# Scaling of the third normalisation as 32 ScalarE instructions a chunk instead of one VectorE instruction

## The chip, the core and the metric

The kernel runs on one core of a Trainium2 chip. The metric is the device time of one execution in microseconds (us), the median of several runs. The engines of the core are TensorE (PE), VectorE (DVE), ScalarE (ACT), GpSimd (POOL) and SyncE (SP, which only issues transfers). Each engine works through its own list of instructions in the order in which they are written and stops at a wait until the semaphore has reached the count that is asked for.

## The reference, cut to what matters

Four residual layers work on an input of 256 images, 256 channels and 7 x 7 positions in float32, each on a group-normalised copy of its input (32 groups of 8 channels):

```
x = x + L0(gn(x))      # 1x1 convolution with gathered rows of the weight
x = x + L1(gn(x))      # linear attention over heads, 5x5 depthwise convolution, projection
x = x + L2(gn(x))      # spatial gate: arg max, gaussian, sigmoid
x = x + L3(gn(x))      # attention over the 49 positions of an image
def gn(v): (g - mean(g)) / sqrt(var(g) + 1e-5)   # for each image and each group
```

The change concerns the last `gn`: `z3 = (x3 - mean3) * rstd3`, whose result feeds L3 (its products f, g and hh, and the residual term).

## The kernel before, in words

Channels lie on partitions (KT = 2 tiles of 128). A chunk is NB = 16 images, COLS = 784 columns a tile (49 positions by 16 images), so that one full tensor of a chunk is 128 x 1568. There are 16 chunks. The first two phases (set-up, L0 and L1) are not touched. The third phase, `gate_and_attention_phase`, does L2 and L3 as a software pipeline that is written out by hand: body r runs the steps of chunk r for `intake`, r-1 for `norm2`, r-2 for `gate`, r-3 for `norm3`, r-4 for `attend` and r-5 for `leave`, for r from 0 to 20. So `norm3` is in bodies 3 to 18 and `attend` in bodies 4 to 19; body 18 has `norm3` and `attend` but neither `norm2` nor `gate`. The order of the work is the order of the `run(...)` lines in `v_body`, `pe_body`, `a_body` and `g_body`.

The third normalisation goes: `v_sum` (DVE sums x3), `pe_stat` (PE spreads the sums over groups), `v_mean`, `v_centre` (zc[1] = x3 - mean, L995), `a_square` (ACT), `v_square_sum` (L1008), `pe_stat`, `v_var` (L1012), `g_root` (POOL raises to the power -0.5, L1436), and `v_scale` (L1023), which writes z3, one of two buffers. In each chunk rstd is 128 x 2 tiles x 16 images: one value for each partition, tile and image.

Who reads z3: `pe_fg` of the next body (L1267, its first step), `pe_hh` (L1290) and the identity products of `pe_out` (L1307). Near the place of the change the orders are:

- DVE, end of a body: `v_x3`, `v_scale` of z2, `v_gap`, `v_scale` of z3, `v_x4` part 0 (L1160, waits for `pe_out` part 0). Then, in the next body: `v_sum` of x3 (L982), `v_hot` (L1043 on, waits for ACT's s_sb), `v_x4` part 1, `v_mean` (L988, waits for `pe_stat`).
- ACT, end of a body: `a_exp` (L1391), `a_hh` 1 and 2, `a_sim_square`, `a_tanh` (L1373, the gate), `a_hh` 3 (L1398), `a_beta` (L1404, two instructions), `a_sums` (L1352, s_sb).
- PE, end of a body: `pe_gate` (L1225), `pe_hh` 3 (L1290), `pe_turn` (L1300, first half after `a_hh` 2, second half after `a_hh` 3), `pe_out` 0, `pe_sums` (L1219), `pe_out` 1; next body: `pe_fg`, `pe_gap` (L1219), `pe_stat` (L1204) for the means, `pe_hot` and so on.
- POOL: `g_root` of norm3, `g_deviation` (L1448), `g_root` of norm2, `g_gapped` (L1443).

Of the kernel before, what the change touches and what calls it, by code (L numbers as in the profile page):

```python
# [13 lines left out]
S = HW * HW  # L14
NB = 16
# [3 lines left out]
KT = C // 128  # L19
# [15 lines left out]
def settle(eng, met):  # L35


    eng.sem_inc(met, 1)
# [787 lines left out]
def gate_and_attention_phase(nc, bass, mybir, W, x2, out, ins, chunks):  # L826
# [10 lines left out]
    ACT = mybir.ActivationFunctionType  # L837
# [5 lines left out]
    with ctx:  # L843
        def sb(name, shape):
            return ctx.enter_context(nc.sbuf_tensor(name, shape, f32))
# [12 lines left out]
        def normed(it, k):  # L858

            return x2_in if k == 0 else x3[it % 3]  # L860

        def scaled(it, k):

            return z2 if k == 0 else z3[it % 2]

        x4 = sb("x4", [128, KT, COLS])
        zc = [sb("zc2", [128, KT, COLS]), sb("zc3", [128, KT, COLS])]
        z2 = sb("z2", [128, KT, COLS])
        z3 = [sb("z3_0", [128, KT, COLS]), sb("z3_1", [128, KT, COLS])]
# [4 lines left out]
        rstd = [sb("rstd2", [128, KT, NB]), sb("rstd3", [128, KT, NB])]  # L874
# [63 lines left out]
        def done(ins_, name):  # L938
            return ins_.then_inc(sems[name], 1)

        def wait(eng, name, count):

            if not isinstance(count, int) or count > 0:
                eng.wait_ge(sems[name], count)

        def by_image(ap):
            return ap.rearrange("p t (b s) -> p t b s", b=NB)

        def over_positions(ap):
            return ap.unsqueeze(3).to_broadcast([128, KT, NB, S])  # L950
# [15 lines left out]
        def two_images(ap, n):  # L966

            return ap[:, PR * n:PR * n + PR]
# [22 lines left out]
        def v_centre(v, it, k):  # L991
            wait(v, f"mean{k + 2}", it + 1)

            wait(v, f"z{k + 2}", it)
            done(v.tensor_tensor(by_image(zc[k][:, :, :]), by_image(normed(it, k)[:, :, :]),  # L995
                                 over_positions(mean[k][:, :, :]), ALU.subtract), f"centred{k + 2}")
            if k == 0:

                wait(v, "gapm", it)
                done(v.scalar_tensor_tensor(gapc[:, :], stat[0][:, :], 1.0 / S,  # L1000
                                            mean[0][:, :, :].rearrange("p t b -> p (t b)"),
                                            ALU.mult, ALU.subtract), "gapc")
# [12 lines left out]
        def v_scale(v, it, k):  # L1015
            wait(v, f"rstd{k + 2}", it + 1)
            if k == 0:

                wait(v, "gated", 2 * it)
            else:  # L1020

                wait(v, "o_mm", 4 * it - 4)
            done(v.tensor_tensor(by_image(scaled(it, k)[:, :, :]), by_image(zc[k][:, :, :]),  # L1023
                                 over_positions(rstd[k][:, :, :]), ALU.mult), f"z{k + 2}")

        def v_then(v, it, ins_, name):

            done(ins_, name)
            wait(v, name, it + 1)
# [133 lines left out]
        def v_body(v, intake, norm2, gate, norm3, attend, leave):  # L1163

            def run(step, chunk, *more):
                if chunk is not None:
                    step(v, chunk, *more)

            run(v_sum, norm3, 1)
            run(v_hot, gate)  # L1170
            run(v_x4, leave, 1)
            run(v_mean, norm3, 1)
            run(v_mean, norm2, 0)
            run(v_centre, norm3, 1)
            run(v_picked, gate)
            run(v_centre, norm2, 0)
            run(v_square_sum, norm3, 1)
            run(v_dist, gate)
            run(v_var, norm3, 1)
            run(v_max, attend)  # L1180
            run(v_dsum, gate)
            run(v_sim, gate)
            run(v_spread_of_sim, gate)
            run(v_square_sum, norm2, 0)
            run(v_context, gate)
            run(v_var, norm2, 0)
            run(v_probs, attend)
            run(v_sum, intake, 0)
            run(v_x3, gate)
            run(v_scale, norm2, 0)  # L1190
            run(v_gap, norm2)
            run(v_scale, norm3, 1)
            run(v_x4, attend, 0)


# [63 lines left out]

        def pe_fg(pe, it):  # L1260

            wait(pe, "z3", it + 1)

            wait(pe, "x4_ok", 2 * it - 1)
            for t in range(KT):
                for h in range(2):
                    mm = pe.matmul(p_a[2 * G * h:2 * G * h + 2 * G, 0, 0:HALF], W["wqk"][:, t, :],  # L1267
                                   z3[it % 2][:, t, HALF * h:HALF * h + HALF], start=(t == 0), stop=(t == KT - 1))
            done(mm, "fg_mm")
# [9 lines left out]

        def pe_hh(pe, it, n):  # L1280

            wait(pe, "z3", it + 1)
            if n < 2:

                wait(pe, "x4_ok", 2 * it)
            else:
                wait(pe, "hh_ev", 4 * it + n - 1)
            for q in range(2):
                for t in range(KT):
                    mm = pe.matmul(p_b[0:PR, n % 2, C * q:C * q + C], two_images(z3[it % 2][:, t, :], 2 * n + q),  # L1290
                                   W["wv"][:, t, :], start=(t == 0), stop=(t == KT - 1))
                done(mm, "hh_mm")
# [114 lines left out]
        def a_body(a, intake, norm2, gate, norm3, attend, leave):  # L1407
            def run(step, chunk, *more):
                if chunk is not None:
                    step(a, chunk, *more)  # L1410

            run(a_fg, attend)
            run(a_gap, gate)
            run(a_square, norm3, 1)
            run(a_hh, attend, 0)
            run(a_square, norm2, 0)
            run(a_gauss, gate)
            run(a_exp, attend)
            run(a_hh, attend, 1)
            run(a_hh, attend, 2)  # L1420
            run(a_sim_square, gate)
            run(a_tanh, gate)
            run(a_hh, attend, 3)
            run(a_beta, attend)
            run(a_sums, norm2)


        def g_root(g, it, k):

            wait(g, f"var{k + 2}", it + 1)  # L1430

            wait(g, f"z{k + 2}", it)
            if k == 0:
                wait(g, "gapm", it)
            settle(g, sems["met_g"])
            done(g.tensor_tensor(rstd[k][:, :, :].rearrange("p t b -> p (t b)"), var[k][:, :], W["minus_half"][:, :],  # L1436
                                 ALU.pow), f"rstd{k + 2}")
# [86 lines left out]
        @block.scalar  # L1524
        def _(a):
            done(a.activation(log_norm[:, :], W["theta"][:, 2:3], ACT.Ln), "logged")
            a.wait_ge(sems["params"], 5)
            bodies(a, a_body)
# [6 lines left out]
def program(nc, ins, out, chunks, n_classes):  # L1535
    import concourse.bass as bass
    from concourse import mybir
    from contextlib import ExitStack
    f32 = mybir.dt.float32
    x2 = nc.dram_tensor("x2_scratch", (chunks, 128, KT, COLS), f32, kind="Internal").ap()  # L1540
    xpart = nc.dram_tensor("x1_scratch", (chunks, 128, KT, COLS), f32, kind="Internal").ap()
    qt = nc.dram_tensor("qkv_scratch", (2, PR, NP, 3 * C), f32, kind="Internal").ap()
    agg = nc.dram_tensor("agg_scratch", (2, NP, 3 * C, PR), f32, kind="Internal").ap()
    ctx = ExitStack()
    with ctx:
        W = {}
        for name, shape in (
            ("w_qkv", [128, KT, 3 * C]), ("w_proj", [128, 4, C]), ("wv", [128, KT, C]), ("wqk", [128, KT, 64]),
            ("w_sub", [128, KT, C]), ("b_sub", [128, KT]), ("mask8", [128, 128]), ("mask_vo", [128, VO]),
            ("ident", [128, 128]), ("image_of", [PR, 2]), ("bn_scale", [128, KT]), ("bn_shift", [128, KT]),  # L1550
            ("g_par", [64, 4]), ("theta", [64, 3]), ("gamma", [128, 1]),
            ("minus_half", [128, KT * NB]), ("plus_half", [64, NB // 2]),
        ):
            W[name] = ctx.enter_context(nc.sbuf_tensor(name, shape, f32))
        setup_phase(nc, bass, mybir, ins, W, n_classes)
        layer_one_phase(nc, bass, mybir, ins, W, (qt, agg, xpart, x2), chunks)
        gate_and_attention_phase(nc, bass, mybir, W, x2, out, ins, chunks)
# [90 lines left out]
```

## Time and profile before

| what | value |
|---|---|
| median of 3 runs | 2461.83 us (2460.21, 2461.83, 2505.93) |
| the profiled execution | 2472.42 us, its span 2470.6 us |
| PE busy | 1950.4 us (79%) |
| DVE busy | 1413.4 us (57%) |
| ACT busy | 928.5 us (38%) |
| POOL busy | 274.7 us (11%) |
| mean granted TensorE clock | 0.898 of full speed |

The shares are averages over two very different parts. In 40 slices of the span DVE is busy five tenths or less up to about 70% of the span (set-up, L0 and L1), and eight or nine tenths in the last 30%, which is the phase that the change touches: it begins near 1755 us and a body of it takes some 41 us in the middle. PE is busy seven tenths there, ACT two to three.

### The profile page before, as it was taken

What the parts mean: (1) busy time and instruction counts of PE and PEld (TensorE: products, weight loads), DVE (VectorE), ACT (ScalarE), POOL (GpSimd) and SP (SyncE); (2) the same over time, 40 slices, a digit from 0 to 9 for tenths busy, and PEclk for the clock granted to TensorE, in tenths of its full rate; (3) what the DMA queues carried; (4) which work ended last, traced back from release to release, by engine and by line L of the source; (5) the groups of instructions that cost most, each with busy time, mean ns of one, the idle gap of its engine ahead of it and who ended that gap; (6) DMA issues with size and microseconds to landing.
All of it is one profiled execution on the core that took longest, in us unless ns stands there. A gap on an engine that the chain in (4) does not pass through costs nothing. (4 is left out here: it accounts for less than half of the span.)

```text
span 2470.6 us, 40333 instructions
## 1 busy us (share of the span) xinstructions
PE 1950.4 (79%) x15572; PEld 1244.2 (50%) x15572; DVE 1413.4 (57%) x2847; ACT 928.5 (38%) x2181; POOL 274.7 (11%) x77
## 2 busy tenths in 40 slices
PE   2788888889999899978687888888436877676768
PEld 1344444445555565556566666666114444343435
DVE  4556565655545545322222244444489989899984
ACT  0344443444444444433333344444113232323232
POOL 1000000000000000000000000000143434343430
PEclk9889999999999999988888899999658888888889
DMA  2111112264675763788889755553111121212101
GB/s 90 51 67 66 66 66 79 80 149 108 180 188 152 198 181 103 194 197 203 214 194 213 191 144 132 131 132 93 70 52 53 53 66 53 66 53 66 56 36 40
DMA packets 258675, 279.42 MB, mean 113 GB/s; under 512 B 207092, under 2 KB 233076, under 8 KB 254392
## 3 DMA queue, kind: packets, MB, share of 16 engines
q1 hardware_dynamic: 258328, 276.58, 41.1%
q8 instruction: 128, 2.10, 0.3%
q14 instruction: 59, 0.48, 0.1%
q0 software_dynamic: 160, 0.26, 0.0%
HBM read 161.21 MB, written 115.61 MB: 112 GB/s over the span
## 5 line engine op out<-in xcount | busy, mean ns | idle before, releaser
L484 DVE TENSOR_TENSOR vk<-p_vk,mask_vo 128x512 f32<-128x512 f32 x256 | 177.1, 692 | 725.1 <-PE p_vk L378 725.0
L1436 POOL TENSOR_TENSOR rstd<-var,minus_half 128x32 f32<-128x32 f32 x32 | 173.9, 5435 | 2062.3 <-DVE var L1012 2062.3
L414 PE MATMUL p_dw<-tw,qd 98*64 98x98 f32 x3072 | 244.6, 296 | 95.9 <-DMA tw<-in_w_toep 56.5
L414 PEld LDWEIGHTS p_dw<-tw,qd 98*64 98x64 f32 x3072 | 200.2, 205 | 151.9 <-issue 48.2
L624 ACT ACTIVATE agg_out<-p_dw 128x294 f32<-128x294 f32 x256 | 106.5, 416 | 317.3 <-PE p_dw L414 294.1
L597 ACT ACTIVATE half_b<-p_qkv 98x384 f32<-98x384 f32 x256 | 125.8, 491 | 258.6 <-PE p_qkv L337 258.4
L337 PE MATMUL p_qkv<-w_qkv,half_a 128*98 128x384 f32 x512 | 198.0, 535 | 0.0
L437 PE MATMUL p_g<-o,w_proj 128*128 128x392 f32 x512 | 195.6, 506 | 0.5 <-ACT o L632 0.5
L337 PE MATMUL p_qkv<-w_qkv,z_odd 128*98 128x384 f32 x512 | 187.8, 512 | 0.0
L390 PE MATMUL p_out<-vk,qr 128*49 128x136 f32 x2048 | 170.7, 287 | 1.3 <-DVE oN L499 1.1
L616 ACT ACTIVATE qr<-p_turn 128x196 f32<-128x196 f32 x256 | 85.4, 334 | 197.1 <-PE p_turn L347 116.5
L1290 PE MATMUL p_b<-wv,z 128*98 128x256 f32 x512 | 147.7, 446 | 0.4 <-ACT hh L1398 0.4
L430 PE MATMUL p_g<-half_a,w_sub 128*128 128x392 f32 x256 | 107.3, 548 | 36.3 <-DVE half_a L549 36.3
L632 ACT ACTIVATE o<-p_turn 128x196 f32<-128x196 f32 x256 | 85.4, 334 | 116.1 <-PE p_turn L399 115.5
L337 PEld LDWEIGHTS p_qkv<-w_qkv,half_a 128*98 128x98 f32 x512 | 88.7, 184 | 73.2 <-issue 73.2
L1204 PE MATMUL p_wide<-stat,mask 128*128 128x32 f32 x128 | 27.4, 317 | 119.6 <-DVE stat L1008 83.4
L1290 PEld LDWEIGHTS p_b<-wv,z 128*98 128x98 f32 x512 | 96.2, 196 | 48.7 <-issue 16.5
L390 PEld LDWEIGHTS p_out<-vk,qr 128*49 128x49 f32 x2048 | 111.6, 126 | 16.6 <-issue 1.7
L378 PEld LDWEIGHTS p_vk<-vT,kT 98*32 98x32 f32 x4096 | 70.6, 109 | 97.4 <-issue 65.8
L337 PEld LDWEIGHTS p_qkv<-w_qkv,z_odd 128*98 128x98 f32 x512 | 84.6, 176 | 67.2 <-issue 67.2
L437 PEld LDWEIGHTS p_g<-o,w_proj 128*128 128x128 f32 x512 | 91.2, 193 | 53.3 <-issue 14.1
L603 ACT ACTIVATE vT<-half_b,image_of 98x256 f32<-98x256 f32 x256 | 114.7, 498 | 0.0
(179 smaller groups left out, 3294.3 us busy)
## 6 DMA issues: line engine op xcount, KB each, us to landing
qkv_scratch<-half_b SPq DMA_DIRECT2D x32, 1176.0 KB
qd<-qkv_scratch SPq DMA_DIRECT2D x16, 2352.0 KB
agg_scratch<-agg_out SPq DMA_DIRECT2D x64, 588.0 KB, 7.1
tw<-in_w_toep SPq DMA_DIRECT2D x128, 220.5 KB
x_scratch<-xb SPq DMA_DIRECT2D x32, 784.0 KB, 5.3
half_a<-agg_scratch SPq DMA_DIRECT2D x48, 392.0 KB, 6.4
half_b<-agg_scratch SPq DMA_DIRECT2D x48, 392.0 KB, 6.0
half_a<-in_x SPq DMA_DIRECT2D x16, 784.0 KB, 4.5
```

The lines of the kernel that those rows point to most:

```text
L337: mm = pe.matmul(p_qkv[r][0:PR, 0:QKV], z[c % 2][:, t, PR * w:PR * w + PR], W["w_qkv"][:, t, QKV * e:QKV * e + QKV], start=(t == 0), stop= ...
L390: mm = pe.matmul(out_of[64 * i:64 * i + S, pr, 0:VO], qr[:, G % 4, at:at + S], vk[:, G % 2, pr, i, :], start=True, stop=True)
L414: mm = pe.matmul(p_dw[NP * cp:NP * cp + NP, PR * s:PR * s + PR], qd[:, QB % 2, :, ch - QB_CH * qb], tw[:, SB % 2, :, 6 * (F % SB_FILLS) + ...
L430: mm = pe.matmul(bank[:, 0:HALF], W["w_sub"][:, t, 128 * m:128 * m + 128], y[:, t, HALF * h:HALF * h + HALF], start=(t == 0), stop=(t == K ...
L437: mm = pe.matmul(bank[:, 0:HALF], W["w_proj"][:, q0 + e, 128 * m:128 * m + 128], o[:, n % 2, e, HALF * h:HALF * h + HALF], start=(e == 0), ...
L484: v.tensor_tensor(dst[:, :, 0:128].rearrange("p k (c n) -> p k c n", c=HC), src[:, :, 0:2 * D].unsqueeze(2).to_broadcast([128, 4, HC, 2 * D]),
L597: a.activation(raw[:, e, w, :], p_qkv[r][0:PR, 0:QKV], ACT.Copy).then_inc(raw_ev, 1)
L603: a.activation(vT[:, G % 2, :, i, :, 0:2 * D], src.rearrange("r q (c n) -> r q c n", c=HC), ACT.Copy, scale=W["image_of"][:, i:i + 1]).the ...
L616: a.activation(qr[:, G % 4, :], p_turn[:, 0:2 * PR], ACT.Relu).then_inc(qr_ok, 1)
L624: a.activation(agg_out[:, DB % 2, at:at + 3, :].rearrange("p s n -> p (s n)"), p_dw[:, 0:3 * PR], ACT.Copy).then_inc(dw_ev, 1)
L1290: mm = pe.matmul(p_b[0:PR, n % 2, C * q:C * q + C], two_images(z3[it % 2][:, t, :], 2 * n + q), W["wv"][:, t, :], start=(t == 0), stop=(t ...
L1436: done(g.tensor_tensor(rstd[k][:, :, :].rearrange("p t b -> p (t b)"), var[k][:, :], W["minus_half"][:, :], ALU.pow), f"rstd{k + 2}")
```

## The change

The step `v_scale` for norm3 is taken out of DVE's list. A new step `a_scale3(t)` on ACT does the same product in 16 instructions for each tile t, one for each image: a copy of 128 x 49 elements with a scale that is read from one column of rstd. Tile 0 is placed between `a_tanh` and `a_hh` 3, tile 1 between `a_beta` and `a_sums`. The semaphore z3 now counts KT * NB = 32 for a chunk instead of 1; `pe_fg`, `pe_hh`, `v_centre` and `g_root` wait for the new counts.

```
         def v_centre(v, it, k):
-            wait(v, f"z{k + 2}", it)
+            wait(v, f"z{k + 2}", it if k == 0 else KT * NB * it)
...
+        def a_scale3(a, it, t):
+            if t == 0:
+                wait(a, "rstd3", it + 1)
+                wait(a, "o_mm", 4 * it - 4)
+            for b in range(NB):
+                done(a.activation(z3[it % 2][:, t, S * b:S * b + S], zc[1][:, t, S * b:S * b + S], ACT.Copy,
+                                  scale=rstd[1][:, t, b:b + 1]), "z3")
...
             run(v_gap, norm2)
-            run(v_scale, norm3, 1)
             run(v_x4, attend, 0)
...
         def pe_fg(pe, it):
-            wait(pe, "z3", it + 1)
+            wait(pe, "z3", KT * NB * (it + 1))
...
         def pe_hh(pe, it, n):
-            wait(pe, "z3", it + 1)
+            wait(pe, "z3", KT * NB * (it + 1))
...
             run(a_tanh, gate)
+            run(a_scale3, norm3, 0)
             run(a_hh, attend, 3)
             run(a_beta, attend)
+            run(a_scale3, norm3, 1)
             run(a_sums, norm2)
...
         def g_root(g, it, k):
-            wait(g, f"z{k + 2}", it)
+            wait(g, f"z{k + 2}", it if k == 0 else KT * NB * it)
```

## Rows read from the trace of the kernel before

**Rows 1.** Line 1023 by source: duration ns min/median/max, first and last start.

```profile
L1023 DVE TENSOR_TENSOR z<-zc,rstd x32: 1781/1784/1792, 1773.9 to 2436.7; 128x1568 f32<-128x1568 f32 x32
```

**Rows 2.** Chain that ended last, in order of time: start us, us, what; one body.

```profile
2074.04 5.37 POOL rstd L1436
...
2082.11 0.72 ACT gate L1373
...
2085.95 3.11 PE p_b L1290 x8
2089.08 0.61 ACT hh L1398
...
2101.09 0.58 PE p_wide L1204 x4
2101.80 1.78 DVE zc L995
```

**Rows 3.** Timeline of DVE, same body: start, us, instructions, [idle before <-releaser].

```profile
2091.37 1.78 DVE L1023 TENSOR_TENSOR z<-zc,rstd 128x1568 f32<-128x1568 f32 x1
2093.50 0.97 DVE L1160 TENSOR_TENSOR x<-p_a,x 128x784 f32<-128x784 f32 x1 [0.35 <-PE p_a L1310]
...
2096.09 0.54 DVE L1043 TENSOR_REDUCE best<-s_sb 64x8 f32<-64x392 f32 x1
...
2101.47 0.41 DVE L988 TENSOR_SCALAR mean<-p_wide 128x32 f32<-128x32 f32 x2 [1.59 <-PE p_wide L1204]
```

**Rows 4.** Timeline of ACT, same body, the places where the new steps go.

```profile
2089.08 0.60 ACT L1398 ACTIVATE hh<-p_b 98x512 f32<-98x512 f32 x1 [6.25 <-PE p_b L1290]
...
2090.31 0.50 ACT L1404 ACTIVATE beta<-p_b 98x392 f32<-98x392 f32 x1 [0.24 <-PE p_b L1300]
2094.95 0.49 ACT L1352 ACTIVATE s_sb<-p_group 64x392 f32<-64x392 f32 x1 [4.14 <-PE p_group L1219]
```

**Rows 5.** Timeline of PE: the first reader of z3, and one product at two clocks.

```profile
2068.06 2.83 PE L1219 MATMUL p_group<-prod,sel 128*32 128x392 f32 x8 [2.86 <-DVE prod L1082]
...
2098.11 1.54 PE L1267 MATMUL p_a<-z,wqk 128*64 128x392 f32 x8
2099.58 1.51 PE L1219 MATMUL p_group<-gapped,sel 128*32 128x392 f32 x8
```

**Rows 6.** Timeline of ACT: its smallest instructions of this phase, one after the other.

```profile
2073.77 0.39 ACT L1361 ACTIVATE dist<-dist,inv_scale 64x112 f32<-64x112 f32 x1 [2.52 <-DVE dist L1072]
2074.19 0.39 ACT L1363 ACTIVATE gauss<-dist,log_norm 64x112 f32<-64x112 f32 x1
2074.95 1.98 ACT L1391 ACTIVATE sc<-p_a,neg_max 98x98 f32<-98x98 f32 x8 [0.38 <-DVE neg_max L1146]
```

**Rows 7.** Groups of ACT by form over the span: busy us, mean ns | idle before.

```profile
L1348 ACT ACTIVATE sq<-zc 128x1568 f32<-128x1568 f32 x32 | 48.3, 1510 | 92.6 <-DVE zc L995 92.6
...
L649 ACT ACTIVATE std<-var 128x32 f32<-128x32 f32 x32 | 7.2, 224 | 6.3 <-DVE var L532 6.3
```

**Rows 8.** Timeline of DVE where body 3 ends.

```profile
1846.32 1.78 DVE L1023 TENSOR_TENSOR z<-zc,rstd 128x1568 f32<-128x1568 f32 x1
...
1849.76 0.55 DVE L1043 TENSOR_REDUCE best<-s_sb 64x8 f32<-64x392 f32 x1
```

**Rows 9.** Timeline of ACT, same place.

```profile
1849.23 0.49 ACT L1352 ACTIVATE s_sb<-p_group 64x392 f32<-64x392 f32 x1 [10.60 <-PE p_group L1219]
```

**Rows 10.** Timeline of all engines in body 18 and at the start of body 19.

```profile
2431.26 5.44 POOL L1436 TENSOR_TENSOR rstd<-var,minus_half 128x32 f32<-128x32 f32 x1 [24.37 <-DVE var L1012]
...
2436.76 0.60 ACT L1398 ACTIVATE hh<-p_b 98x512 f32<-98x512 f32 x1 [1.63 <-PE p_b L1290]
...
2437.41 0.54 PE L1300 MATMUL p_b<-ident,sc 98*98 98x98 f32 x4 [0.35 <-ACT hh L1398]
...
2437.99 0.50 ACT L1404 ACTIVATE beta<-p_b 98x392 f32<-98x392 f32 x1 [0.24 <-PE p_b L1300]
...
2444.18 1.54 PE L1267 MATMUL p_a<-z,wqk 128*64 128x392 f32 x8
```

**Rows 11.** Busy time and PEclk of a stretch: PE, PEld, DVE, ACT, POOL, clock, DMA, GB/s.

```profile
2068.00:2072.00 4.00, 3.22 (x11) 0.97 (x12) 3.90 (x7) 1.51 (x1) 0.00 (x0) 0.59 0.34 58
```

**Rows 12.** Chain that ended last, body 5: the first p_b product after the gate.

```profile
1920.16 3.66 PE p_b L1290 x8
```

## The prediction

> **What bounds the kernel now.** The page says that DVE is 80 to 90% busy in the phase that the change touches, which invites the sum "one instruction of 1.78 us less on the busiest engine, in 16 chunks". The first view to read is therefore not a share but the chain that ended last, over one body in the middle. It goes from DVE's centring through the first half of the body to POOL's root, on to the gate on ACT, then to PE's p_b product, ACT's copy of hh, and from there along PE to the p_wide product, which releases DVE's next centring [rows 2]. L1023 is not on it: from 2085.95 to 2101.67 the body belongs to PE, with one ACT copy between. The second view is DVE's own timeline over that stretch [rows 3]: right behind z3 DVE waits 0.35 us for PE's p_a, and before the mean it waits another 1.59 us for PE's p_wide. An engine that waits for PE directly behind the instruction that is removed gains nothing when that instruction goes. The third view is ACT's timeline, which shows the two holes that the new steps are put into [rows 4]: 6.25 us between the gate and hh, 4.14 us between beta and s_sb. The fourth is the beginning and the end of the phase, where bodies are incomplete and the holes may be absent [rows 8 to 10].
>
> **The change, part by part.**
>
> *Removed from DVE:* 16 of the 32 instructions of L1023, each 1784 ns [rows 1]; busy time falls by 16 x 1.78 = 28.5 us. In the shown body z3 starts at 2091.37. Without it DVE stands at x4 part 0 some 1.7 us sooner, but that waits for p_a and still starts at 2093.50; its idle time grows from 0.35 to about 2.05 us [rows 3]. What follows on DVE does not move. Saved on the path: 0 in bodies 4 to 17. In body 3, where nothing attends yet, the chain does run through z3 at 1846.32. But DVE's best, two instructions on at 1849.76, needs ACT's s_sb, which ends at 1849.23 + 0.49 = 1849.72 whatever DVE does [rows 8, 9]: saved at most 0.04 us. So the removal is worth 0, and PE's wait is what covers it.
>
> *Added to ACT:* 32 copies of 128 x 49 a chunk, 512 in all. No row shows this form. Four rows bound it. The eight exponentials of 98 x 98, each with its own bias column, take 1.98 us together: 0.25 us each. Two instructions of 64 x 112, the second of which waits for the first, start 0.42 us apart [rows 6]. An instruction of 128 x 32 out of and into SBUF takes 224 ns, and 1568 columns take 1510 ns, so a column costs (1510 - 224) / 1536 = 0.84 ns [rows 7]; 49 columns are then 0.24 us. I take 0.24, since the SBUF row of 32 columns is nearest in size and the exponentials, nearest in kind (independent, back to back, a pointer operand, a semaphore count each), say the same. 16 of them are 3.8 us. The ends are 0.20 (the exponentials less 49 columns at 0.84 ns) and 0.42, so 3.2 to 6.7 us for a tile.
>
> *Tile 0, bodies 4 to 17:* rstd3 is ready at 2074.04 + 5.37 = 2079.41, before the gate ends at 2082.83 [rows 2], so the new wait costs nothing. Behind the new instructions on ACT stand hh, beta and s_sb; for hh PE waits. The hole is 6.25 us [rows 4], 0.39 us an instruction: at 0.24 the step ends 2.4 us before hh is due. Cost 0, covered by PE's gate and p_b products; without that cover it would be the whole 3.8 us. The wait on o_mm asks for products of the body before, done long ago.
>
> *Tile 1, bodies 4 to 17:* from 2090.81 the hole to s_sb is 4.14 us [rows 4], 0.26 us an instruction. At 0.24 it just fits. Beyond 0.26 s_sb comes late, but DVE's best reads it at 2096.09, 0.65 us after it is ready, and behind that lies DVE's 1.59 us before the mean [rows 3], which absorbs a delay too: 4.14 + 0.65 + 1.59 = 6.38 us, 0.40 us an instruction, before the mean is late. The reader of z3 itself, PE's p_a product at 2098.11 [rows 5], is 7.3 us away. Cost 0. The counts that DVE's centring and POOL's root now wait for are reached some 7 and 20 us ahead.
>
> Set against the ScalarE page of the Trainium skill ("ScalarE: Activation LUTs", section "Rules for kernel authors"): it budgets about 0.3 us for an ACTIVATE with a pointer operand plus 0.83 ns an element, and tells authors to leave multiplications to VectorE. By that, as an estimate, a tile would be 16 x 0.34 = 5.5 us. It would still fit hole one, overrun hole two by 1.3 us, of which 0.65 us is free at best and the rest goes into the wait before the mean; only the end of the kernel, below, would cost 1.7 us more. The column price agrees with the 0.84 ns above; the 0.3 us does not agree with 0.25 us an exponential [rows 6].
>
> *Body 18:* here is neither gate nor norm2, and the hole is gone. rstd3 ends only at 2431.26 + 5.44 = 2436.70, and hh, which stands behind the new tile 0 on ACT, started at 2436.76 [rows 10]. Now ACT waits for rstd3, scales 3.8 us, and hh starts near 2440.6. PE's second half of the turn waited for that hh already (0.35 us), and everything to the end hangs on it: **+3.8 us** on the path. Tile 1 starts after beta, near 2438.5 + 3.8 = 2442.3, ends 2446.1, and PE's p_a product, at 2444.18 before, comes at 2448 or later: hidden.
>
> In addition PE stands still for about 4 us instead of 0.35 us. What follows such a stop is shown in the middle of each body: after 2.86 us of waiting the 8 products of L1219 take 2.83 us, at a granted clock of 0.59 (a mix of 1.2 and 2.4 GHz), where the same 8 products in a busy stretch take 1.51 us [rows 5, 11]. I add that difference once, **+1.3 us**; the bounds are 0 (the clock stays up) and 3 us (the outputs of body 18, some 6 us, half of them at the lower level).
>
> **Sum:** 0 + 0 + 3.8 + 1.3 = +5.1 us on the profiled execution's 2472.42, that is 2477.5 us. The median lies 10.6 us below the profiled execution; the same difference on 2461.83 gives **2467 us**, +0.2%.
>
> **The rivals.**
>
> *A, the forecast:* chance 0.73; own range 2464 to 2472, from +3.2 with no clock loss to +6.7 with 3 us of it.
>
> *B, DVE is the bound after all.* If the waits behind z3 were only slack that re-forms further back, each of 15 bodies would be 1.70 us shorter (z3's start after z2's): -25 us, 2437 us. For it: 90% busy, and the first half of the body is DVE's. Against it: the wait for PE directly behind z3 in each full body, and a chain without L1023. 0.05.
>
> *C, slower: the small copies are dear, and hh is late in every body.* Place: tile 0 in front of hh. Point: above 6.25 / 16 = 0.39 us. Price: 14 x (16p - 6.25) + 16p + 1.3 us. At the 0.42 us of the dependent pair it is 14 x 0.47 + 6.7 + 1.3 = 14.6 us, 2476. For 2% (49 us) p must be 0.56 us, more than any ACT row of up to 128 columns above. 0.10, of which 0.02 beyond 2%.
>
> *D, the clock.* PE's p_b product behind the gate takes 3.11 us in the middle of the phase but 3.66 us in body 5 [rows 2, 12]: bodies that do the same work differ by how the low stretch of the clock falls on them. If a shift near body 3 moved it in all 14 full bodies it would be up to 14 x 0.55 = +7.7 us; if the early ones improved, -2 or -3 us. With the 5.1 us: 2464 to 2475. Against it: nothing on PE moves before body 18. 0.12.
>
> **Range and chances.** 2457 to 2480 holds A and D whole and most of C, and a few us for run-to-run spread (two runs before are 1.6 us apart); B and the far end of C are left out. Over 2% means under 2412.6 or over 2511.1, about what a measurement can tell from no change: faster 0.01 (no case reaches it), within 0.96, slower 0.03 (the far part of C and a disturbed median like the run of 2505.93).
>
> **What would show each step.** In the trace after: full bodies still near 41 us; DVE's wait before x4 part 0 near 2 us; ACT's new instructions near 0.24 us apart, tile 0 ended before hh is due; s_sb at its old place to within half a microsecond; in body 18 hh some 3.8 us late behind rstd3, and PE at a lower clock after it. The forecast is wrong if bodies shorten, if they lengthen because hh starts right behind a new copy, or if body 18 costs nothing.

## The result, and the profile after

The changed kernel takes 2475.53 us (median of 16 runs) against 2462.61 us before (16 runs): a ratio of 1.0050, 95% interval 1.0036 to 1.0065, that is +12.3 us with 8.9 to 16. The 12.3 us are the ratio times the time before; one disturbed run of each kernel (3411.15 us after, 2505.93 us before) is in the medians but not in the ratio. The change makes the kernel slower by half a per cent, well inside 2%; the forecast was +5.1 us. The profiled execution took 2480.26 us (span 2478.5), 7.8 us more than the one before; it reached the first centring of the phase at 1758.17 us instead of 1762.09, in a part that is the same in both kernels. So the two traces are compared by stretches of the phase, each from one centring of DVE (L995) to another; the phase itself is 11.8 us longer.

The page after has the new group on ACT (its columns: busy us, mean ns of one, idle before):

```profile
L1031 ACT ACTIVATE z<-zc,rstd 128x49 f32<-128x49 f32 x512 | 118.9, 323 | 1.6 <-POOL rstd L1445 1.6
```

The timeline of ACT over one full body shows both holes of [rows 4] with what now stands in them:

```profile
2077.89 0.71 ACT L1380 ACTIVATE gate<-sim,half_par 64x392 f32<-64x392 f32 x1 [3.54 <-DVE sim L1123]
2078.51 3.72 ACT L1031 ACTIVATE z<-zc,rstd 128x49 f32<-128x49 f32 x16
2085.40 0.60 ACT L1405 ACTIVATE hh<-p_b 98x512 f32<-98x512 f32 x1 [3.17 <-PE p_b L1297]
...
2086.63 0.50 ACT L1411 ACTIVATE beta<-p_b 98x392 f32<-98x392 f32 x1 [0.25 <-PE p_b L1307]
2087.03 3.72 ACT L1031 ACTIVATE z<-zc,rstd 128x49 f32<-128x49 f32 x16
2091.27 0.49 ACT L1359 ACTIVATE s_sb<-p_group 64x392 f32<-64x392 f32 x1 [0.52 <-PE p_group L1226]
```

Sixteen copies take 3.72 us. In front of hh 3.17 us are still free, in front of s_sb 0.52 us: neither is late. The timeline of DVE, the counterpart of [rows 3]:

```profile
2089.82 0.97 DVE L1168 TENSOR_TENSOR x<-p_a,x 128x784 f32<-128x784 f32 x1 [2.59 <-PE p_a L1317]
...
2097.79 0.41 DVE L988 TENSOR_SCALAR mean<-p_wide 128x32 f32<-128x32 f32 x2 [1.59 <-PE p_wide L1211]
```

The wait right behind the place of z3 has grown from 0.35 to 2.59 us, more than the 1.70 that were freed, because in this body PE's products in front of hh ran longer (3.70 us against 3.11 in [rows 2]). PE's timeline:

```profile
2081.66 3.70 PE L1297 MATMUL p_b<-wv,z 128*98 128x256 f32 x8
```

The body shown is body 9 in both traces; it takes 41.56 us after and 40.98 before. Other early bodies differ the other way (body 4: 40.93 after, 41.91 before), and body 15 takes 40.96 us in both. Nothing was won. Where the time went is seen at the end. ACT and PE in body 18, two timelines, against [rows 10]:

```profile
2433.60 3.73 ACT L1031 ACTIVATE z<-zc,rstd 128x49 f32<-128x49 f32 x16 [1.60 <-POOL rstd L1445]
2437.23 0.57 ACT L1405 ACTIVATE hh<-p_b 98x512 f32<-98x512 f32 x1
```

```profile
2437.86 0.89 PE L1307 MATMUL p_b<-ident,sc 98*98 98x98 f32 x4 [3.93 <-ACT hh L1405]
2438.54 1.56 PE L1314 MATMUL p_a<-z,ident 128*128 128x392 f32 x2
2439.90 1.87 PE L1317 MATMUL p_a<-beta,hh 98*128 98x98 f32 x8
...
2450.74 2.88 PE L1274 MATMUL p_a<-z,wqk 128*64 128x392 f32 x8
```

The same products of body 18 before, from PE's timeline:

```profile
2437.80 0.93 PE L1307 MATMUL p_a<-z,ident 128*128 128x392 f32 x2
2438.56 1.03 PE L1310 MATMUL p_a<-beta,hh 98*128 98x98 f32 x8
```

And the clock in that part of the trace after (start and end of the stretch, its length, then PE, PEld, DVE, ACT, POOL busy; granted clock; DMA; GB/s), where 0.50 is 1.2 GHz and 1.00 is 2.4:

```profile
2435.00:2437.00 2.00, 0.00 (x0) 0.00 (x0) 0.00 (x0) 2.00 (x10) 0.00 (x0) 0.94 0.00 0
2439.00:2441.00 2.00, 2.00 (x8) 1.44 (x7) 0.00 (x0) 2.00 (x10) 0.00 (x0) 0.50 0.03 8
2438.00:2453.00 15.00, 15.00 (x52) 10.79 (x52) 1.95 (x2) 4.30 (x18) 0.00 (x0) 0.50 0.03 10
```

ACT waits 1.60 us for rstd3, copies for 3.73 us, and only then takes hh; PE stands still for 3.93 us, its clock falls, and it stays at 1.2 GHz although PE is busy without a gap until the p_a product ends at 2453.62. The ledger, all from starts and ends in the two traces:

| stretch | before | after | difference |
|---|---|---|---|
| bodies 4 to 17 (centring to centring) | 572.1 | 572.5 | +0.4 |
| body 18: centring to start of hh 3 | 11.55 | 15.15 | +3.6 |
| start of hh 3 to end of the p_a product | 8.96 | 16.39 | +7.4 |
| end of the p_a product to end of span | 24.89 | 24.84 | -0.1 |

The remaining 0.4 us of the phase's 11.8 lie ahead of body 4.

### The profile page after: what moved, and what is told of

Same layout as the page of the kernel before. It is cut to its first block and busy times, and to the rows that moved or that the text cites. A ratio compares the mean times of both kernels' runs of the same rounds, so it can differ in the third digit from the quotient of the medians.

```text
span 2478.5 us, 40829 instructions
## 1 busy us (share of the span) xinstructions
PE 1955.6 (79%) x15572; PEld 1248.0 (50%) x15572; DVE 1386.6 (56%) x2831; ACT 1044.3 (42%) x2693; POOL 254.0 (10%) x77
## 3 DMA queue, kind: packets, MB, share of 16 engines
q1 hardware_dynamic: 258328, 276.58, 40.9%
## 5 line engine op out<-in xcount | busy, mean ns | idle before, releaser
L616 ACT ACTIVATE qr<-p_turn 128x196 f32<-128x196 f32 x256 | 85.4, 334 | 197.4 <-PE p_turn L347 116.4
L632 ACT ACTIVATE o<-p_turn 128x196 f32<-128x196 f32 x256 | 85.4, 334 | 116.0 <-PE p_turn L399 115.3
L1297 PEld LDWEIGHTS p_b<-wv,z 128*98 128x98 f32 x512 | 97.1, 198 | 49.0 <-ACT z L1031 15.5
L1031 ACT ACTIVATE z<-zc,rstd 128x49 f32<-128x49 f32 x512 | 118.9, 323 | 1.6 <-POOL rstd L1445 1.6
L390 PEld LDWEIGHTS p_out<-vk,qr 128*49 128x49 f32 x2048 | 111.2, 126 | 16.5 <-issue 1.8
```

Of the source, the lines that this page charges most:

```text
L390: mm = pe.matmul(out_of[64 * i:64 * i + S, pr, 0:VO], qr[:, G % 4, at:at + S], vk[:, G % 2, pr, i, :], start=True, stop=True)
L616: a.activation(qr[:, G % 4, :], p_turn[:, 0:2 * PR], ACT.Relu).then_inc(qr_ok, 1)
L1031: done(a.activation(z3[it % 2][:, t, S * b:S * b + S], zc[1][:, t, S * b:S * b + S], ACT.Copy, scale=rstd[1][:, t, b:b + 1]), "z3")
```

## The experiments

Each was timed beside the kernel before on the same chip. The "tail" is the stretch in its trace from the centring of body 17 to the end of the span: 82.2 us before, 93.2 us after. "Bodies" is the stretch of bodies 4 to 17: 572.1 and 572.5. Body 17 (36.8 us) is in both columns. The column "us" is the ratio times the time before. The expectations of e3b and e6 count the tail to DVE's last instruction, 3.8 us sooner: 78.3 before and 89.3 after.

| run | ratio, 95% interval | us | bodies | tail |
|---|---|---|---|---|
| e1 last chunk on DVE | 0.9985 (0.9969 to 1.0000) | -3.7 | 572.9 | 82.2 |
| e2 before, hh late in body 18 | 1.0036 (1.0018 to 1.0053) | +8.9 | 572.9 | 93.2 |
| e3 20 products in the stop | 1.0043 (1.0024 to 1.0063) | +10.6 | 572.9 | 93.3 |
| e3b 6 products in the stop | 1.0013 (0.9997 to 1.0029) | +3.2 | 572.2 | 85.7 |
| e4 removal alone | 0.9983 (0.9965 to 1.0001) | -4.2 | 569.0 | 82.2 |
| e5 both tiles before hh 3 | 1.0101 (1.0067 to 1.0134) | +24.9 | 583.1 | 92.2 |
| e6 hh late by half | 1.0008 (0.9989 to 1.0027) | +2.0 | 573.5 | 85.6 |
| e7 reordered, z3 on ACT | 1.0079 (1.0054 to 1.0104) | +19.5 | 578.8 | 97.7 |
| e8 reordered, z3 on DVE | 1.0079 (1.0057 to 1.0102) | +19.5 | 578.6 | 97.7 |
| e9 both tiles behind beta in body 18 | 1.0007 (0.9991 to 1.0022) | +1.7 | 572.1 | 85.4 |
| e10 PE filled, z3 on DVE | 0.9933 (0.9915 to 0.9950) | -16.5 | 552.4 | 78.8 |
| e11 PE filled, z3 on ACT | 0.9959 (0.9941 to 0.9977) | -10.1 | 557.2 | 83.1 |

**e1, the last chunk on DVE.** In `a_scale3` and in `v_body`:

```
+            if it == chunks - 1:
+                return
...
             run(v_gap, norm2)
+            run(v_scale_last, norm3)     # as v_scale, last chunk alone, counts 32
```

> The changed kernel, but z3 of the last chunk (body 18) is scaled by DVE in one instruction as before; the other 15 chunks stay on ACT. Theory T (all the loss is in body 18: hh 3.6 us late behind rstd3, then TensorE at 1.2 GHz to the end of the body): the last body is as before, so the time is that of the kernel before, within 2 us, and from the last centring to the end of the span 48 us become some 41 plus the store. Theory U (each of the 14 full bodies loses 0.5 to 0.9 us by the copies or the clock): the loss stays at 8 us or more. Theory B (DVE gives something back in each body): faster than before by up to 25 us.

The loss is gone with one chunk of 16 changed (the 48 and 41 us in the expectation were misread: from the last centring to the end of the span it is 56.4 us after and 45.4 here and before). The tail is that of before and the bodies keep their length with z3 on ACT. Theory U falls, and B with it. The median is 3.7 us under the kernel before, with an interval that ends at 1.0000; the trace has no stretch that is shorter, so nothing is claimed from it.

**e2, the delay alone.** The kernel before with this in front of `a_hh` 3:

```
+        def a_fill(a, it):
+            if it == chunks - 1:
+                wait(a, "rstd3", it + 1)
+                for b in range(NB):       # 16 copies into sq[0], which is free then
```

> The kernel before, z3 on DVE throughout, with 16 small ACT copies into an unused tile in front of hh 3 in body 18 alone, behind a wait for rstd3. Theory T: this alone gives the whole loss of the change, +11 to +13 us: hh about 3.6 us late, PE idle near 4 us, then the second half of the turn, the outputs and the p_a product (7.9 us before) at 1.2 GHz in some 15 us. If the clock counted for little: +3.8 us. Theory U: at most +4 us.

The tail is 93.2 us, that of the changed kernel to a tenth, without any other part of the change; the median is +8.9 us (4.4 to 13). PE's timeline repeats what it did after:

```profile
2428.76 0.89 PE L1300 MATMUL p_b<-ident,sc 98*98 98x98 f32 x4 [3.93 <-ACT hh L1398]
2429.45 1.56 PE L1307 MATMUL p_a<-z,ident 128*128 128x392 f32 x2
...
2441.64 2.88 PE L1267 MATMUL p_a<-z,wqk 128*64 128x392 f32 x8
```

So 11.0 us in the trace come from one late instruction, in one body.

**e3 and e3b, PE kept busy.** The changed kernel, between the halves of `pe_turn`, with 20 and then 6 in `range`:

```
+                if h == 1 and it == chunks - 2:
+                    for r in range(6):
+                        pe.matmul(p_group[0:G, 0, 0:HALF], sel[:, 0, :], ...)   # read by nobody
```

> The changed kernel; while PE waits for the late hh in body 18 it computes 20 products of 128 x 392 that nobody reads (between the halves of the turn). hh stays 3.6 us late. Theory T: the granted clock stays at 1.00, the last body loses 3.6 to 4 us and no more, so the time is 7 to 8 us under the changed kernel and 4 to 5 us over the one before. If the slow outputs had another cause than PE's stop (the copies on ACT, for one), the time is that of the changed kernel.

> As e3_pe_kept_busy, where 20 products took 13.35 us (two passes each, 0.33 us a pass) and not 3.9, so that it kept the clock at 1.00 but added 10 us of its own. Now 6 products, 4.0 us, the length of PE's stop. Theory T: the clock stays at 1.00 through the outputs of body 18 and only the 3.6 to 4 us of the late hh are left: from the first centring of body 17 to the end of the span 82 to 83 us, against 89.3 in the changed kernel and 78.3 before; in the median 7 us under the changed kernel. If the low clock came from ACT's copies and not from PE's stop: no change from 89.3.

In e3 the filler was mis-sized: a float32 product shows as two passes, 20 of them took 13.35 us instead of 4, and its time says nothing; only that the clock stayed at 1.00. In e3b the filler fits the stop. PE's timeline:

```profile
2427.22 4.14 PE L1307 MATMUL p_group<-z,sel 128*32 128x392 f32 x12
2431.28 0.54 PE L1311 MATMUL p_b<-ident,sc 98*98 98x98 f32 x4
2431.66 0.86 PE L1318 MATMUL p_a<-z,ident 128*128 128x392 f32 x2
2432.36 1.03 PE L1321 MATMUL p_a<-beta,hh 98*128 98x98 f32 x8
```

and its clock:

```profile
2430.00:2434.00 4.00, 4.00 (x22) 2.38 (x20) 0.00 (x0) 3.68 (x15) 0.00 (x0) 1.00 0.00 0
```

ACT still copies during the outputs (3.68 us busy), hh is as late as in the changed kernel, but the outputs are as fast as before. The tail is 85.7 us: 3.6 more than before, 7.4 less than after. This splits the loss: 3.6 us the late hh, 7.4 the clock. The clock falls here because PE stands still, not because ACT is busy: the two kernels differ in nothing but the six products.

**e6, half the delay.** e2 with `range(NB // 2)`.

> As e2_before_delay18 with 8 copies in place of 16: hh 1.8 us late, PE's stop about 2.1 us instead of 3.9. If the clock's loss grows in proportion to the stop: half of the loss, +5.5 us, 83.8 us from the centring of body 17 to the end. If a stop of 2.1 us is short enough to leave the clock up: +1.8 us, 80.2 us. In proportion to nothing (any stop costs all): +9 us.

PE's stop is 2.12 us and the tail 85.6, +3.4 us: 1.8 of delay and 1.6 of clock. PE's timeline shows the low level over the first products only:

```profile
2428.76 0.54 PE L1300 MATMUL p_b<-ident,sc 98*98 98x98 f32 x4 [2.12 <-ACT hh L1398]
...
2430.31 1.86 PE L1310 MATMUL p_a<-beta,hh 98*128 98x98 f32 x8
...
2433.11 1.03 PE L1310 MATMUL p_a<-beta,hh 98*128 98x98 f32 x8
```

Between two of the three expectations, +1.8 and +5.5 us: a short stop does cost clock, but less than in proportion.

**e9, the copies moved.** In body 18 alone both tiles stand behind `a_beta`.

> The changed kernel; in body 18 alone both tiles stand behind beta, so hh 3 does not wait for rstd3. All scaling stays on ACT. Theory T: hh is on time, PE does not stop there; z3 is complete 7.4 us after beta, some 1.8 us after the p_a product could start, so PE stops about 1.8 us there instead: before +2 us, plus at most 2 us if the clock falls after it. If only the amount of work on ACT mattered: as the changed kernel.

+1.7 us (-2.2 to +5.4), tail 85.4, +3.2 us: hh is on time, PE stops 1.52 us for z3 in front of p_a, and its next long run of hh products takes 9.72 us instead of 8.84. The same copies on the same engine cost less than a third of what they cost in front of hh (3.2 of 11.0 us).

**e5, the cover taken away.** Both tiles in front of `a_hh` 3 in every body.

> The changed kernel with both tiles in front of hh 3 in every body: 32 copies, 7.4 us, in a hole of 6.3 to 6.8 us. Theory T (the hole is the cover, and behind it hh is on the path): each of the 14 full bodies is 0.6 to 1.2 us longer, and body 18 is late by another 3.7 us: 12 to 21 us over the changed kernel. If hh had more room than the forecast says: +3.7 us, from body 18 alone.

ACT's timeline of a full body:

```profile
2158.84 7.33 ACT L1031 ACTIVATE z<-zc,rstd 128x49 f32<-128x49 f32 x32
2166.08 0.57 ACT L1405 ACTIVATE hh<-p_b 98x512 f32<-98x512 f32 x1
```

hh now starts right behind the last copy. The 14 bodies are 11.0 us longer than before, 0.8 each, within the 0.6 to 1.2 that were expected from the size of the hole. The time is +24.9 us (16.5 to 33, from four runs), 12.6 over the changed kernel. In body 18 PE stands still 7.5 us, but the low clock behind it costs only 2.0 us (from PE's restart behind hh to the end of p_a 10.3 instead of 8.3), so the tail is 92.2, less than after. The stop is twice as long as in the changed kernel and the clock's part a quarter.

**e4, the removal alone.** DVE scales one image of z3 only, ACT gets nothing.

```
-            done(v.tensor_tensor(by_image(scaled(it, k)[:, :, :]), ...
+                done(v.tensor_scalar(z3[it % 2][:, 0, 0:S], zc[1][:, 0, 0:S], rstd[1][:, 0, 0:1], None, ALU.mult), "z3")
```

> The removal alone: in the kernel before, DVE scales only the first image of z3 (128 x 49, about 0.2 us instead of 1.78), the rest of z3 stays at zeros written once at the start of the phase; nothing is added to ACT. The attention is then computed on other data. Theory T (PE's wait covers L1023): 0 to -2 us, DVE's wait in front of x4 part 0 grows from 0.35 to about 1.9 us. Theory B (DVE bounds the bodies): -20 to -25 us.

```profile
2121.88 0.24 DVE L1023 TENSOR_SCALAR z<-zc,rstd 128x49 f32<-128x49 f32 x1
2123.99 0.97 DVE L1162 TENSOR_TENSOR x<-p_a,x 128x784 f32<-128x784 f32 x1 [1.87 <-PE p_a L1312]
```

DVE's timeline: 1.54 us less work, 1.52 us more waiting, as forecast (1.9). The body of that time is 40.96 us, as before. -4.2 us with an interval that touches 1.0001; the 3.1 us fewer in "bodies" lie in the early ones: bodies 4 to 9 took 40.9 each here, while in each other trace with the body's order of before some of them took 41.5 to 42.4, with z3 on either engine (rival D). That the early bodies differ by the clock and not by the removal is argued from those other traces, not tested. Theory B's -20 to -25 is excluded.

**e7 and e8, a shorter path.** `v_body` and `a_body` reordered, with z3 on ACT (e7, last chunk on DVE) and on DVE (e8):

```
             run(v_picked, gate)
-            run(v_centre, norm2, 0)
             run(v_square_sum, norm3, 1)
             run(v_dist, gate)
             run(v_var, norm3, 1)
-            run(v_max, attend)
+            run(v_centre, norm2, 0)
...
             run(v_var, norm2, 0)
+            run(v_max, attend)
```

> Built on e1_last_on_dve. The path of a body runs through the first half of DVE's list, so two steps that the gate does not need leave it: the maximum of the scores goes behind the variance of norm2 (ACT's exponentials behind the tanh), and the centring of norm2 behind the variance of norm3, so that POOL's root starts earlier. Of the 32 copies 8 stand before hh 3 and 24 behind beta. Theory T: the gate is ready 1.05 us sooner in each of 14 full bodies, which DVE's waits at the end of the body (2.6 and 1.6 us) can give: -15 us against e1. If POOL's root or another wait takes its place: 0.

> The same new order built on the kernel before, with z3 on DVE throughout. DVE then has 1.7 us less room at the end of a body (waits of 0.35 and 1.6 us), which still holds the 1.2 us that x4 part 0 comes late. Theory T: -15 us against the kernel before, the same as on ACT, so that moving z3 to ACT is worth nothing even then. If the room on DVE is what decides: the version with z3 on ACT is 10 us or more faster than this one.

Wrong, in sign: +19.5 us, both. Timelines of DVE and POOL in e8:

```profile
2102.70 1.77 DVE L995 TENSOR_TENSOR zc<-x,mean 128x1568 f32<-128x1568 f32 x1
...
2111.40 0.16 DVE L1113 TENSOR_SCALAR sstd<-sstd 64x8 f32<-64x8 f32 x1 [0.61 <-POOL sstd L1448]
...
2115.61 0.97 DVE L1150 TENSOR_REDUCE ssm<-sc 98x8 f32<-98x784 f32 x1 [2.04 <-ACT sc L1391]
```

```profile
2102.99 6.79 POOL L1436 TENSOR_TENSOR rstd<-var,minus_half 128x32 f32<-128x32 f32 x1 [15.40 <-DVE var L1012]
```

POOL's root, now beside DVE's centring, takes 6.79 us instead of 5.44 [rows 10], and DVE, which had hidden the exponentials behind other work, waits 2.04 us for them. Bodies 4 to 15 take about 41.8 us each in both. In both traces the chain that ended last goes through that wait to z of norm2, and from there over PE's sums of it (L1219) to the next mean: it leaves DVE just ahead of z3, so that z3's engine makes no difference here either. It is close, though: in e8 DVE has no wait left from the exponentials to the next centring, where in e7 it still waits 1.68 us before the mean. The tail is 15.5 us longer. In both of its last bodies PE stands still 3.14 us until DVE has scaled the exponentials, which now come late on ACT, and in body 18 the first groups of output products behind the stop take 1.87 us instead of 1.03; what each part costs was not separated.

**e10 and e11, the low clock in each body.** Before the second statistics product of norm2 PE stands still 5.6 us in every body with a gate, and the gate's products and hh 3 then run at a mean granted clock of 0.55 (2082 to 2089 us before). Seven products that nobody reads go there:

```
+        def pe_fill(pe, it):
+            wait(pe, "sim_max", it + 1)
+            for r in range(7):
+                pe.matmul(p_group[0:G, 0, 0:HALF], sel[:, 0, :], ...)
...
+            run(pe_fill, gate)
             run(pe_stat, norm2, 0, 1)
```

> The kernel before, with 7 products of 128 x 392 (two passes of 0.33 us each, 4.7 us in all, read by nobody) in PE's 5.6 us stop in front of the second statistics product of norm2, in each of the 16 bodies with a gate. They should keep TensorE at 2.4 GHz for the gate's products and for hh 3, which would be 2.65 us sooner (the products 1.5 instead of 3.0 us, hh 3 1.94 instead of 3.1). With z3 on DVE only the waits of DVE behind it can be given back, 0.35 + 1.59 = 1.9 us a body: -27 us in all. If the clock stays low all the same: 0.

> The same 7 products on e1_last_on_dve (z3 on ACT but for the last chunk), 8 of the 32 copies before hh 3 and 24 behind beta, since the hole before hh 3 shrinks to 3.6 us. Here DVE's waits are 2.6 and 1.6 us, so the whole 2.65 us of PE can be given back: -37 us against the kernel before, 10 us faster than e10. That would be the place where the change is worth something: with PE out of the way DVE bounds the end of the body. If DVE does not bound it even then, both are the same.

e10 is the fastest kernel of the study, -16.5 us (12 to 21 less), 0.67% under the kernel before and some 29 us under the changed one. PE's timeline of a body in which the filler holds the clock, beside [rows 2]:

```profile
2106.22 4.80 PE L1297 MATMUL p_group<-z,sel 128*32 128x392 f32 x14
...
2112.08 0.93 PE L1225 MATMUL p_wide<-gate,spread 32*128 32x392 f32 x4 [0.73 <-ACT gate L1380]
2112.82 0.85 PE L1225 MATMUL p_group<-gate,spread 32*128 32x392 f32 x4
2113.60 1.97 PE L1290 MATMUL p_b<-wv,z 128*98 128x256 f32 x8
```

That body is 39.3 us long; in the body before it p_b still took 3.73 us behind the same filler, and it was 41.2. Over 14 bodies the gain is 19.7 us of the 27 expected; ahead of body 4 the kernel loses 2.7 us, which leaves 17.0 for the phase. e11 was to be 10 us faster than e10 and is not; its best body is 39.3 us as well. Further on in the same body of e10, PE's timeline shows why:

```profile
2120.80 1.51 PE L1219 MATMUL p_group<-z,sel 128*32 128x392 f32 x8 [0.81 <-DVE z L1023]
```

PE now waits for z of norm2, which DVE makes just ahead of z3, and the chain that ended last leaves DVE there, with z3 on either engine. DVE bounds these bodies, but not behind z3, so moving z3 cannot shorten them. In the longer bodies PE comes last, as before. The two kernels also differ otherwise: the clock falls in other bodies in e11, its other order of copies (8 and 24) brings s_sb up to 1.3 us late, for which DVE waits 0.31 to 0.56 us in nine bodies, and from the centring of body 18 on e11 is 2.6 us longer.

## Why the prediction was right or wrong

- *The removal from DVE, 0 on the path:* right. DVE's wait grew in its place (after: 2.59 us; e4: 1.87), and a body of 40.96 us is 40.96 or 40.97 in before, after, e1 and e4. The chain and the wait behind the instruction told more than the 90% of busy time.
- *The price of a copy, 0.24 us:* 3.72 us for 16, 0.23 each; the sum had 3.8. Taking the start-to-start distance of the exponentials instead of a duration mattered: the page's mean is 323 ns for one, and 16 x 0.323 would be 5.2 us, yet they overlap. The estimate of 0.34 us from the Trainium skill ("ScalarE: Activation LUTs", section "Rules for kernel authors") is near the duration of one and too high for sixteen in a row.
- *Tile 0 and tile 1 in bodies 4 to 17, 0:* right, +0.4 us over 14 bodies in the trace. The point of 0.39 us an instruction was confirmed from the other side by e5: 7.3 us in the hole lengthen each body by 0.8.
- *Body 18, +3.8 us by the late hh:* right, 3.6 in the trace, 3.6 in e3b.
- *The clock, +1.3 us with a bound of 3:* this is the term that was mis-sized. It measured 7.4 us (after and e2), against 1.6 behind a stop of 2.1 us (e6) and 2.0 behind one of 7.5 us (e5). The prediction priced it by one group of products at a mean clock of 0.59 [rows 5, 11] and bounded it by "half of the outputs", as if the low level had to end while PE was busy with the outputs; here all outputs and the p_a product, nearly 16 us of busy PE, ran at 1.2 GHz. The bound should have been the whole busy stretch at half speed, 8 us.
- *The rivals:* B is excluded by e1 and e4. C did not occur; its mechanism is real (e5), its price per copy was not. The forecast's own range, rival A with 2464 to 2472, missed: its ends, +3.2 and +6.7 us, give 2465 to 2468.5, and +12.3 lies outside both. D's spread is visible in every trace: bodies 4 to 17 take 569.0 to 573.5 us in the kernels whose bodies have the order and the cover of before, independent of z3's engine.
- *The total:* 2467 forecast, 2475.5 measured, inside the range of 2457 to 2480; +5.1 against +12.3, and 6.1 of the 7.2 us between them are the clock term. That the total falls inside is partly luck: the upper end was put at 2480 for the rivals C and D, and neither of them made the loss. The phase of the two profiled executions differs by 11.8 us, the medians by 12.9, the ratio says 12.3.

What stays open is why the clock stayed low for nearly 16 us behind a stop of 3.9 us and for 5 us or less behind stops of 2.1 and 7.5 us. The runs show it depends on more than the stop's length; e2 repeats the long one with the same work before it.

## What to carry to other kernels

Before moving work off a busy engine, look at what that engine does right behind the instruction: if it waits there for another engine, the move is worth nothing, however busy the engine is on average. Then walk through the bodies in which the pipeline is half empty, since the hole that hides the moved work may not exist there; one body of 21 cost the whole difference here, and leaving its chunk on the old engine took it back (e1). And price a new stop of TensorE not by its length alone but also by what all the work behind it would cost at half the clock.

## What the runs showed of the hardware that was not expected

DVE's instructions slow POOL's, and not the other way round: g_gapped (128 x 1568 on POOL) takes 4.30 us beside DVE's two-input z3 and 2.82 us where DVE does not run it (after, e1, e4), and POOL's root of 128 x 32 takes 6.79 instead of 5.44 us when a centring on DVE (1.77 us, two inputs) runs beside it (e7, e8), while the two DVE instructions keep their 1.78 us. The change gave POOL back 1.48 us a body, off the path.

```profile
2087.31 2.82 POOL L1452 TENSOR_TENSOR gapped<-z,gapm 128x1568 f32<-128x1568 f32 x1 [3.71 <-DVE gapm L1045]
```

This row is of the timeline of POOL after. A float32 product of TensorE with 392 columns shows as two passes, at a clock of 1.00 some 0.33 us apart: 12 of them take 4.14 us in the filler of e3b. In the sums over groups of channels, 8 passes take only 1.51 us [rows 5]. There the products come in pairs that write different rows of p_group, and PE's timeline before, cut to the first two passes of such a sum, shows them side by side:

```profile
2093.39 0.52 PE L1219 MATMUL p_group<-z,sel 128*32 128x392 f32 x2
```

Two passes take 0.52 us together, where one alone takes 0.49. The filler writes the same rows each time and so gets no such pair; that the rows decide it is read from the code and was not tested.
